# Four fused image layers on one core: evacuations placed between softmax steps, and the edge columns of an oriented filter dealt out anew

## The reference

```python
# layer 0, on xn = group_norm(x)
q, k, v = (conv2d(xn, w, b, 1) for w, b in ((wq, bq), (wk, bk), (wv, bv)))      # 3x3
bias = conv2d(xn, wb, bb, 3)                                                    # 7x7
attn = einsum('bchw,bcjw->bchj', q, k) / 16.0 + bias
a = softmax(attn, axis=1)                                                       # over channels
x = x + einsum('bchw,bcjw->bchj', v, a)
...
# layer 3, on xn = group_norm(x)
lstd = sqrt(max(avg_pool3(xn * xn) - avg_pool3(xn) ** 2, 1e-6))                 # local deviation
lstd = (lstd - min) / (max - min + 1e-8)                                        # per channel
theta = (sample % 8) * pi / 8
center = conv21x21(xn, gauss(3.65, 3.65 / 8, theta))                            # depthwise
surround = conv21x21(xn, gauss(3 * 3.65, 3 * 3.65 / 8, theta))
x = x + max(center - lstd * surround, 0)
```

## Time and profile before

| | |
|---|---|
| median of 3 runs | 1190.22 (1189.51 to 1196.2) |
| profiled execution | 1189.9, of which the span 1188.1 |
| busy, share of the span | PE 92%, DVE 68%, ACT 45%, POOL 27% |
| mean granted TensorE clock | 0.977 of full |
| attention stage | to about 605 |
| filter stage on PE | 892.4 to 1182.1 |

### The profile page before, as it was taken

One profiled execution on the slowest core, in us unless ns is written; L12 is line 12 of the kernel. 1 busy time (PEld: TensorE's weight loads), 2 busy tenths in 40 slices (PEclk: granted clock), 3 DMA queues, 4 the chain that ended last, 5 costly groups with the idle time before them and its releaser, 6 DMA issues.

```text
span 1188.1 us, 38670 instructions
## 1 busy us (share of the span) xinstructions
PE 1087.3 (92%) x17124; PEld 792.1 (67%) x17124; DVE 804.2 (68%) x994; ACT 536.8 (45%) x747; POOL 323.1 (27%) x364
## 2 busy tenths in 40 slices
PE   2999999999999999999993589887989999999997
PEld 2999999989999899999951245332434444444443
DVE  6456486684857848567287988689988645466444
ACT  3524736546365553645344967677931211111110
POOL 1374446535465354644510000023300000000000
PEclk9999999999999999999995989989999999999999
DMA  6020020200202001010001445323354654566551
GB/s 210 8 77 4 3 77 3 77 3 3 77 3 77 3 3 41 3 41 4 3 2 44 102 102 130 75 64 74 93 141 134 192 171 107 170 173 193 154 140 42
DMA packets 52116, 89.79 MB, mean 76 GB/s; under 512 B 8795, under 2 KB 36699, under 8 KB 50940
## 3 DMA queue, kind: packets, MB, share of 16 engines
q1 hardware_dynamic: 44264, 80.56, 24.3%
q10 hardware_dynamic: 7700, 6.89, 2.0%
HBM read 36.89 MB, written 11.99 MB: 41 GB/s over the span
## 4 chain that ended last, share of the span: by engine, by line
PE 69%; DVE 19%; issue 4%; ACT 3%; DMA 3%; SPq 2%; DVEq 0%; ACTq 0%
PE psum L1511 35%; PE psum L1764 15%; PE psum L1775 10%; PE psum L1664 4%; DVE small L703 3%; DMA arena<-arena 2%; PE psum L1566 2%; DVE small L586 1%; DVE arena L1000 1%; DVE small L665 1%; DVE psum L664 1%; PE psum L1579 1%; DVE X L896 1%; PE psum L1713 1%; SPq L501 1%
## 5 line engine op out<-in xcount | busy, mean ns | idle before, releaser
L1511 PE MATMUL psum<-arena 128*128 128x64 f16 (+2 forms) x11904 | 513.9, 207 | 23.8 <-DMA arena<-arena 12.6
L1511 PEld LDWEIGHTS psum<-arena 128*128 128x128 f16 x11904 | 496.7, 98 | 39.3 <-issue 12.7
L625 DVE TENSOR_TENSOR arena<-psum,arena 128x512 f32<-128x512 f32 x128 | 87.2, 689 | 177.3 <-PE psum L1511 147.1
L1764 PE MATMUL psum<-arena 128*128 128x512 f16 (+2 forms) x936 | 191.8, 366 | 0.0
L1764 PEld LDWEIGHTS psum<-arena 128*128 128x128 f16 x936 | 92.0, 98 | 97.9 <-issue 2.0
L1423 POOL TENSOR_SCALAR arena<-arena,constants_f 128x256 f16<-128x256 f16 x126 | 138.9, 1130 | 0.0
L1419 POOL TENSOR_TENSOR arena<-arena 128x256 f16<-128x256 f32 x63 | 51.6, 819 | 307.8 <-ACT arena L1181 307.8
L1775 PE MATMUL psum<-arena 120*128 120x512 f16 (+1 forms) x528 | 116.9, 379 | 0.6 <-DMA arena<-edge_columns 0.6
L1176 ACT ACTIVATE arena<-arena 128x256 f16<-128x256 f32 x63 | 26.3, 417 | 195.8 <-issue 105.4
L1775 PEld LDWEIGHTS psum<-arena 120*128 120x128 f16 (+1 forms) x528 | 51.3, 97 | 62.6 <-issue 1.0
L1467 POOL TENSOR_TENSOR arena<-arena 128x1024 f32<-128x1024 f32 x16 | 30.4, 1900 | 203.8 <-ACT arena L1323 150.9
(11 more groups left out here) (211 smaller groups left out, 1428.7 us busy)
## 6 DMA issues: line engine op xcount, KB each, us to landing
arena<-in_filter_tables SPq DMA_DIRECT2D x8, 1280.0 KB, 9.0
arena<-arena SPq DMA_DIRECT2D x32, 264.0 KB, 3.9
X<-in_x SPq DMA_DIRECT2D x16, 512.0 KB, 4.6
arena<-arena SPq DMA_DIRECT2D x32, 256.0 KB, 3.9
out<-X SPq DMA_DIRECT2D x16, 512.0 KB, 4.0
arena<-edge_columns SPq DMA_DIRECT2D x90, 80.0 KB
arena<-edge_columns ACTq DMA_DIRECT2D x70, 80.0 KB
arena<-arena SPq DMA_DIRECT2D x32, 140.0 KB, 2.5
```

Source lines behind the costliest of these rows:

```text
L625: v.tensor_tensor(out_, bank_rows(k), biasrow, ALU.add).then_inc([g.staged0, g.staged1][k], 1)
L1511: last = mm(conv[k][:, c0:c1], win[:, kk, lx, y + e, dx:dx + W, :].rearrange("p w s -> p (w s)"), wt[:, lw, d, w0:w1], start=(n == 0), sto ...
L1764: mm(bank[4 * s + 2 * f + hf][:, C * lo:C * hi], tb[:, f, d + 2, lt], xt[s][:, hf, lx, YP + d + lo:YP + d + hi].rearrange("p y c -> p (y c)"),
```

## The change

In the attention body the subtraction of the maximum becomes a function of its own, `softmax_shift`, and the two evacuations of row 1 are placed one ahead of it and one behind it. In the filter stage the samples are laid out in another order on the host, so that turn t has orientation ORDER[t]; the host puts the results back in order. For each orientation the 240 edge lines of a half are dealt out anew between the two edge windows (`EDGE_NEAR`, `EDGE_FAR`; an entry is a row offset with a run of lines, or with a block of rows and columns), 112 to 128 partitions in each. By the tables of the host, windows in use go from 154 to 142. Orientations 0, 1 and 7 have their lines in DRAM ordered by column (`BY_COLUMN`). Each entry is one DMA: 7, 9, 13, 14, 13, 10, 10 and 7 per half and sample in the eight turns. The loops over turns on SP and ACT are written out.

```diff
+BY_COLUMN = (0, 1, 7)
+ORDER = (2, 4, 1, 0, 7, 3, 5, 6)
+SAMPLES = [o + NT * s for s in range(2) for o in ORDER]
+EDGE_NEAR = {
+    0: ((1, 0, 20), (2, 0, 20), (3, 0, 20), (4, 0, 20), (5, 0, 20), (0, 2, 2, 0, 5), (6, 0, 2, 0, 5)),
+    1: ((1, 0, 8), (2, 0, 12), (3, 0, 20), (4, 0, 28), (5, 0, 30), (6, 0, 2, 0, 7)),
+    2: ((1, 0, 40), (2, 0, 40), (3, 0, 40)),
+    3: ((2, 20, 15), (3, 0, 40), (4, 0, 40), (5, 0, 30)),
+    4: ((2, 10, 30), (3, 0, 40), (4, 0, 40), (5, 0, 10)),
+}
+EDGE_FAR = {
...
+    4: ((0, 20, 20), (1, 0, 40), (2, 0, 10), (5, 10, 30), (6, 0, 20)),
+}
...
+def edge_line(t, row, column):
+
+    row = G - 1 - row if t > NT // 2 else row
+    return G * column + row if t in BY_COLUMN else NBW * row + column
...
+        def edge_pieces(t, s, h):
+
+            line = 2 * YN * C
+            for k, part in enumerate(edge_parts(ORDER[t], h)):
+                at_ = 0
+                for a, lines in part:
+                    n = sum(len(run) for run in lines)
+                    src = edge_dram[s, h, lines[0][0]:lines[0][-1] + 1, :, C * a:C * (a + NY)]
+                    if len(lines) > 1:
+                        src = bass.AP(edge_dram.tensor, src.offset,
+                                      [[G * line, len(lines)], [line, len(lines[0])], [YN * C, 2], [1, C * NY]])
+                    yield edges[s][at_:at_ + n, k, h], src
+                    at_ += n
...
-                        sp.dma_start(edge_dram[s, h, NBW * r:NBW * r + NBW],
+                        first, last = edge_line(ORDER[t], r, 0), edge_line(ORDER[t], r, NBW - 1)
+                        sp.dma_start(edge_dram[s, h, first:last + 1:(last - first) // (NBW - 1)],
...
-                    for part, at_, r0, n, a in ((0, 0, 0, 4, 1), (0, 4, 0, 4, 2), (0, 8, 0, 4, 3),
-                                                (1, 0, 0, 4, 4), (1, 4, 0, 4, 5), (1, 8, 0, 2, 6), (1, 10, 2, 2, 0)):
-                        sp.dma_start(edges[s][NBW * at_:NBW * (at_ + n), part, h],
-                                     edge_dram[s, h, NBW * r0:NBW * (r0 + n), :, C * a:C * (a + NY)]
-                                     ).then_inc((edge_in if h == 0 else right_in)[s], 16)
+                    for dst, src in edge_pieces(t, s, h):
+                        sp.dma_start(dst, src).then_inc((edge_in if h == 0 else right_in)[s], 16)
...
                 link(v.tensor_reduce(mx, att_hc, AX.X, ALU.max))
+
+            def softmax_shift(j):
                 v.tensor_tensor(prob_ch, att_ch, over_channels(mx), ALU.subtract).then_inc(g.shifted_ready, 1)
...
                 softmax_a(j)
-                evacuate_rows(i, 1, 2)
+                evacuate(i, 1, 0)
+                softmax_shift(j)
+                evacuate(i, 1, 1)
                 softmax_sum(j)
...
+                for dst, src in edge_pieces(t, s, 1):
+                    a.dma_start(dst, src).then_inc([g.right_in0, g.right_in1][s], 16)
...
-            with a.Fori(0, NT - 2) as t:
+            for t in range(NT - 2):
                 high(t + 1, 0)
...
+                    near, far = (edge_count(part) for part in edge_parts(ORDER[t], hf))
+                    used = [v for v in (5, 6 + 2 * hf, 7 + 2 * hf) if filled[t, f, v]]
+                    for window in used:
+                        rows = {5: P, 6 + 2 * hf: near, 7 + 2 * hf: far}[window]
...
-                pe.wait_ge([g.edge_in0, g.edge_in1][s], 16 * 7 * (t + 1))
-                pe.wait_ge([g.right_in0, g.right_in1][s], 16 * 7 * (t + 1))
+                pe.wait_ge([g.edge_in0, g.edge_in1][s], edge_loads(t, 0))
+                pe.wait_ge([g.right_in0, g.right_in1][s], edge_loads(t, 1))
```

More of the change, by code:

```diff
@@ L50, with edge_parts, edge_count, edge_rows @@
 NPS = 3
-NREAL = 12 * NBW
 KB, KQ, KV, KK = range(4)
 NSIDE, NCENT = 256, 640
+BY_COLUMN = (0, 1, 7)
+ORDER = (2, 4, 1, 0, 7, 3, 5, 6)
+SAMPLES = [o + NT * s for s in range(2) for o in ORDER]
+EDGE_NEAR = {
[5 rows of a table added]
+}
+EDGE_FAR = {
[5 rows of a table added]
+}
+def edge_line(t, row, column):
+    row = G - 1 - row if t > NT // 2 else row
+    return G * column + row if t in BY_COLUMN else NBW * row + column
+def edge_parts(t, hf):
+    parts = []
+    for part in (EDGE_NEAR[min(t, NT - t)], EDGE_FAR[min(t, NT - t)]):
+        pieces = []
+        for a, *of in part:
+            if len(of) == 2:
+                lines = [range(of[0], of[0] + of[1])]
+                if hf:
+                    lines = [range(40 - of[0] - of[1], 40 - of[0])]
+            else:
+                r0, c0 = of[0], of[2]
+                if hf:
+                    r0, c0 = G - of[0] - of[1], NBW - of[2] - of[3]
+                lines = [range(G * c + r0, G * c + r0 + of[1]) for c in range(c0, c0 + of[3])]
+            pieces.append((6 - a if (t > NT // 2) != (hf == 1) else a, lines))
+        parts.append(pieces)
+    return parts
+def edge_count(part):
+    return sum(len(run) for a, lines in part for run in lines)
+def edge_rows(t, part):
+    place = {edge_line(t, q, c): (q, c) for q in range(G) for c in range(NBW)}
+    at = [(4 * (a - 3) + place[n][0], place[n][1]) for a, lines in part for run in lines for n in run]
+    return np.array(at).T
 def host_constants():
@@ L72, in host_constants @@
     r, w = p // NH, p % NH
-    j, wi = p // NBW, p % NBW
-    real = p < 12 * NBW
     rows_in, cols_in, used = [], [], []
@@ L78, in host_constants @@
     rows_in.append(np.where(r < 2, 12 + r, r - 12)), cols_in.append(w), used.append(p >= 0)
[L79 to L85, removed]
     tab = np.zeros((NT, P, 2, NWIN, 2, P), np.float16)
     for t in range(NT):
-        th = float(np.float32(t * np.pi / NT))
+        th = float(np.float32(ORDER[t] * np.pi / NT))
         xr = xx * np.cos(th) + yy * np.sin(th)
         yr = -xx * np.sin(th) + yy * np.cos(th)
+        del rows_in[6:], cols_in[6:], used[6:]
+        for hf in range(2):
+            for part in edge_parts(ORDER[t], hf):
+                rows, cols = edge_rows(ORDER[t], part)
+                unused = np.zeros(P - len(rows), int)
+                rows_in.append(np.concatenate([rows, unused]))
+                cols_in.append(np.concatenate([cols, unused]) + (NH if hf == 0 else -NBW))
+                used.append(p < len(rows))
         for cs, m in enumerate((1.0, 3.0)):
@@ L385, in win3, with edge_loads @@
             return 0 <= tap <= 2
+        def edge_pieces(t, s, h):
[10 more added lines that the diff above has]
+                    at_ += n
+        def edge_loads(t, h):
+            return 16 * sum(len(part) for turn in range(t + 1) for part in edge_parts(ORDER[turn], h))
         @block.sync
@@ L543, in _ @@
             load_tables(1, 1)
[L545 to L551, removed]
+            for t in range(NT - 2):
+                for s in range(2):
+                    prefetch(t + 1, s)
+                    store_out(t, s)
+                load_tables(t + 2, t % 2)
             for s in range(2):
@@ L1768, in rest_of @@
                 def rest_of(f, hf):
[L1769 to L1772, removed]
+                    near, far = (edge_count(part) for part in edge_parts(ORDER[t], hf))
+                    used = [v for v in (5, 6 + 2 * hf, 7 + 2 * hf) if filled[t, f, v]]
+                    for window in used:
+                        rows = {5: P, 6 + 2 * hf: near, 7 + 2 * hf: far}[window]
+                        src = outer[s][:, hf] if window == 5 else edges[s][0:rows, (window - 6) % 2, hf]
                         for lt, lx in ((0, 0), (0, 1), (1, 0)):
-                            rows = src.shape[0]
                             last = mm(bank[4 * s + 2 * f + hf], tb[0:rows, f, window, lt], src[:, lx],
-                                      start=False, stop=(window == 7 + 2 * hf and lt == 1), skip_group_check=True)
+                                      start=False, stop=(window == used[-1] and lt == 1), skip_group_check=True)
                     return last
@@ L1809, in lay_out @@
 def lay_out(x, wq, bq, wk, bk, wv, bv, wb, bb, w1c, b1c, m1, mb1, m2, mb2):
-    rows = x.reshape(B, C, NY, G, W).transpose(3, 1, 0, 2, 4).reshape(P, B, PIX)
+    rows = x[SAMPLES].reshape(B, C, NY, G, W).transpose(3, 1, 0, 2, 4).reshape(P, B, PIX)
     side, cent = np.zeros((G, C, 4, NSIDE), np.float32), np.zeros((G, C, 3, NCENT), np.float32)
@@ L1862 @@
     r = _run(nc, [arrays], core_ids=[0])
-    return r.results[0]["out"].reshape(G, C, B, NY, W).transpose(2, 1, 3, 0, 4).reshape(B, C, H, W)
+    ordered = r.results[0]["out"].reshape(G, C, B, NY, W).transpose(2, 1, 3, 0, 4).reshape(B, C, H, W)
+    return ordered[_np.argsort(SAMPLES)]
```

## The result

| | before | after |
|---|---|---|
| median, us | 1190.89 (14 executions, 1189.51 to 1196.97) | 1200.35 (14 executions, 1197.43 to 1205.08) |
| ratio, with 95% interval | | 1.0071 (1.006 to 1.0083) |
| span of the profiled execution | 1188.1 | 1203.3 |
| mean granted TensorE clock | 0.977 | 0.967 |
| PE busy | 92% | 90% |

The change makes the kernel 0.7% slower, inside the forecast range and 5.35 us above the forecast of 1195. The profiled execution of the changed kernel took 1205.08, the longest of its 14 and 4.73 above their median; 2.4 us of it came in before the filter stage, in layers that the change doesn't touch (the first edge matmul of the stage starts at 894.87 after and 892.45 before).

A forecast was written before the change was run, and what follows sets the result against it. PE, busy 92%, bounds the kernel; after the change ACT's load loop was to set the filter stage's time. 1189.9 + 0.3 (attention) + 4.1 (filter stage) = 1194.3, put at 1195 us, range 1180 to 1208.

The forecast's parts named there:

- Part one's waits: Attention, moved evacuation of row 1: PE's wait of 2.29 us per pair becomes 0.25, 1.83 and 0.49, +0.28.
- Part one as its own rival had it: Attention rival: all 2.29 us gone in five pairs, with both clock drops, 14.7 in all; chance 0.05.
- Part one's clock: Attention: one of two PE clock drops of 1.6 us avoided, bringing the evacuation move to +0.3, bounds -1.3 and +1.9.
- Matmuls removed: Filter stage: edge windows fall from 154 to 142, so 72 matmuls and 15.6 us of PE work less.
- The loop: Filter stage: ACT's rounds grow by 0.80 us per edge load and set the time; end +4.1 us.
- Landing: Filter stage: after the last edge load is out, landing takes 2.33 us and PE 0.14 more.
- The clock behind the waits: Filter stage: new PE waits may lower its clock, costing once 1.6 us at most behind the last wait.
- The floor that decided: Filter stage: latest of the end times set by loads plus remaining PE work, 1186.2 through turn 6, against 1182.1 before.
- PE never waits: Filter stage before the change: PE's row and edge matmuls follow without a gap until 1182.09.
- its own range: Whole kernel: the forecast's range from its terms, 1184 to 1202 us, stretched to 1180 to 1208 for 8 in 10.
- Cheap small loads: Filter-stage rival: smaller edge loads cost ACT 0.65 us or less, PE sets the pace, 1174.6 us; chance 0.18.
- By-column loads cost more: Filter-stage rival: the extra dimension costs up to 0.38 us per load, loop +7.6, 1202 or 1207 us; chance 0.20.

The follow-up runs named there:

- e1: Kernel before with only the moved evacuation of row 1 in attention, filter stage untouched: 1189.53 us against 1191.37, ratio 0.9978.
- e6: Changed kernel with tables of turns 2 to 7 and right-half edge loads of turns 1 to 7 issued from GpSimd: 1178.28 us, ratio 0.9882 to before.
- e3: Changed kernel without the moved evacuation and with the old 7 loads per half, 528 edge matmuls; new order and written-out loops stay: 1192.04 us, ratio 1.0002 to before.
- e4: Kernel with old windows, new turn order and no moved evacuation, loads cut into 7 to 14 plain pieces per half: 1202.52 us, ratio 1.0083 to before.
- e2: Changed kernel with both evacuations of row 1 behind the subtraction again, so the filter change alone: 1200.71 us, ratio 1.0066 to before.
- e5: Changed kernel with tables of turns 2 to 7 issued from GpSimd's queue instead of SP's: 1187.7 us against 1192.62 before, ratio 0.9964.
- e8: Kernel before with every evacuation of rows 1 to 3 one softmax step earlier: 1184.12 us against 1191.64, ratio 0.9929.

## Why the prediction was right, and where its terms were off

**Part one's waits: right.** 0.25, 1.83 and 0.49 were worked out, 0.25, 1.70 and 0.36 came, together 2.31 for the 2.29 of before. The stretch that holds them is 0.38 longer, where +0.28 was forecast. Part one as its own rival had it (all of 2.29 gone) fell.

**Part one's clock: mis-sized.** "I take one of two avoided" gave +0.3 with bounds -1.3 and +1.9; both drops were gone, and e1 gained 2.6. That is outside the bounds, though its interval (0.9965 to 0.999, or 1.2 to 4.2 us) reaches to them, and small beside the range.

**Matmuls removed: right in number** (456 left of 528), and their worth was right too: in e6 the stage is 11.6 shorter, and 15.3 with its one gap and the longer matmuls behind it counted in, for the 15.6 worked out.

**The loop: right.** "ACT's loop sets the time" is what the timeline shows, and e3 and e4 show that the count of loads alone does it, e6 that the issues on ACT are the ones that count. The sum of rounds held well. ACT's loads of the second sample of turn 5 were to be out at 1102.0 and were at 1108.33, 6.3 later: 2.4 of it is the late entry into the stage, and 3.9 is the loop. A load took ACT 0.84 instead of 0.80 (127.4 us for 152 over the 14 rows of ACT's queue), which makes 4.9 over the 118 loads up to there; the rest of the rounds was 1.0 shorter.

**Landing: mis-sized.** "Landing takes 2.33 and PE 0.14 more" was enough for the one first sample that PE waited for: SP's loads, the later ones there, were out at 1009.50 and PE started at 1011.17, 1.67 later. It failed for second samples, where ACT's loads come last: their last loads go out just as SP issues the next table (1107.78 in the timeline), and PE starts 4.6, 6.3 and 6.6 after them. In turn 5 that is 4.2 more than 2.47. The table was costed only as something that the stores queue behind, not as something that lands beside the loads; e2 and e5 are what speaks for that reading. So three of the four gaps stand at second samples, where the prediction put them at first ones; their size of 4 us was right (3.36 to 5.03).

**The clock behind the waits: mis-sized.** "Behind the last wait once 1.6 at most" was 2.87 (8.23 against 5.36 in the timeline for 24 matmuls), and 3.05 against the 5.18 that the prediction's sum has for them. The bound came from a stretch behind a wait of 2.25; these waits were of 3.4 to 5.0. The length of the wait alone doesn't give the price: in e2 the same 24 matmuls took 7.03 behind a wait of 4.07. Behind the three earlier waits it cost nothing at the end, as the prediction had it, since ACT's loop set the pace there.

**The floor that decided.** Through the second sample of turn 5 the prediction's numbers give 1102.0 + 2.47 + 79.1 of PE work = 1183.6, below its latest floor, 1186.2 in turn 6. Measured, with 2.4 of entry, 3.9 of loop, 4.2 of landing and 3.05 of clock on top, that floor was 1197.26 (the chain's last row, 1193.36 + 3.90), within 0.2 of their sum, and became the one that ended last. All four terms are those of the profiled execution; how the 4.73 between it and the median spread over them, no trace shows.

**Readings of rows.** The 0.40 that the prediction gives for "a load of plain rows" is a store's (line 512 writes `out` from X), so the extra 0.38 per by-column load had no load behind it. "PE never waits" in the filter stage leaves out one wait of 0.6, at the first edge matmuls. And "its own range" doesn't follow from its terms: they add up to -6.6 and +13.6 around 1194.3, so 1187.7 to 1207.9, which the stated 1180 to 1208 takes in.

**The rivals.** *Cheap small loads* fell: smaller pieces cost ACT the same, 774 ns at 20, 40 and 80 KB in e4. The Trainium skill (DMA: Bandwidth & Descriptors, Issuing engines are not separate DMA queues) calls the time to initiate a DMA usually small relative to the DMA itself. A single one of these loads agrees with that (0.84 us on average, against 7.29 from the start of the last issue to its landing beside a table), but ten issues in a row took ACT 8.65 us, and ACT's next step stood behind them. *By-column loads cost more* fell too. In the changed kernel ACT's 152 loads, 20 of them by column, took 0.838 on average (the spread of their issue times, in ns, as in e4's row):

```profile
L1430 ACTq DMA_DIRECT2D arena<-edge_columns x152: 628/792/1525, 921.8 to 1175.6; - x152
```

and in e4, without any, 0.823 (125.2 us for 152). The first 14 loads of the turn with most pieces took 11.50, the ten of a turn without by-column pieces 8.33: 0.82 and 0.83 each.

## What to carry to other kernels

Before an edit buys matmuls with DMAs, count the issues on each queue and ask what that engine computes after them: here 72 matmuls (15.6 us) were paid with 0.84 us of ACT per load, and ACT's next step stood behind them. Work the loop out round by round against PE's cover, and for the last round ask what else lands at that moment and at which clock PE will come back. The cure was to move issues off the engine in the loop (e6) and to take every step of a hand-written order one place earlier, not the first one alone (e8).

## What the runs showed of the hardware that had not been expected

GpSimd issued the same 152 loads at a median of 578 ns, ACT at 792. A 1.28 MB load issued on SP's queue at 1107.78 stands beside loads on ACT's queue, issued up to 1108.33, that PE could use only after 6.64 us; with the table on another queue and at another moment it was 2.6 to 3.7 (e5), and 1.70 where the table went out just behind the last load (e2). And behind waits of 3.4 to 5.0 us PE's next 18 to 30 matmuls took 1.68 to 2.90 us longer, at a granted clock of 0.57 to 0.79; behind waits of 1.7 at most in the attention stage it stayed at 1.00.
